# Twelve attention heads laid out as eight on 128 rows and four on 64 rows per image, in a kernel for a vision tower

## The chip, the core and the metric

The kernel runs on one core of one Trainium2 chip. The metric is the device time in microseconds (us) of the whole program. TensorE (PE in the profile) multiplies into eight banks of PSUM. VectorE (DVE), ScalarE (ACT) and GpSimd (POOL) do the work between the products, and SyncE (SP) issues most of the DMAs. The engines run on their own and meet at semaphores.

## What is computed

Sixty-four images of 3x224x224 become 196 tokens of 192 features each. A retention-like attention with twelve heads of 16 features follows (no softmax; the scores are multiplied by a decay with the distance), then a layer norm, a soft mixture of 64 slots with one two-layer expert each, and a last layer norm. Cut to what matters:

```python
h = einsum('bnk,dk->bnd', patches(x), W)                      # 196 tokens, K = 768, D = 192
q, k, v = silu(h @ Wq), silu(h @ Wk), silu(h @ Wv)            # 12 heads of 16
decay = where(i >= j, exp(log_slope[head] * (i - j)), 0)
out = ((q @ k.T) * decay) @ v                                 # per head
out = layernorm((out * sigmoid(h @ Wg1 @ Wg2)) @ Wo) * ln_w + ln_b
h = layernorm(h + out)
xn = rmsnorm(h) * norm_w;  logits = cosine(slots, xn) * scale
y = expert_s(softmax_over_tokens(logits) @ xn)                # 64 experts, 192 -> 768 -> 192
h = layernorm(h + softmax_over_slots(logits) @ y)
```

## The kernel before

The program has three phases. **Phase 1** goes over 32 pairs of images. A step i of it holds three stages of three different pairs: the tokens and the attention of pair i (flag `a`), the output projection and first norms of pair i-1 (`c`), the slot logits and slot inputs of pair i-2 (`d`). All 30 steps from 2 to 31 hold all three; steps 3 to 30 are a hardware loop. **Phase 2** runs the 64 experts, two at a time, with six weight buffers that SP refills. **Phase 3** combines, adds and normalises.

A pair has 392 token columns: two images of 196, each in two tiles of T = 98. The order of the work on each engine is that in which the code of `step` is written for it; nothing reorders it. TensorE's step reads: `embed(i, 0)`, `project_out(i-1, 0)`, `token_features(i-2)`, `embed(i, 1)`, `project_out(i-1, 1)`, `h_turned` with `logits` in it, the products for q, v and k, then the attention with pieces of pair i-2 set between its blocks.

The names that matter:

- Heads: two groups g of six heads (96 rows), so kT and qm are 96 x 2 x 392. An attention block is one (group, image), four to a pair (`ORDER`). `scores` (L1005) has 2 x 3 products, each of 32 rows (two heads, of whose queries `qm` holds one copy with the odd and one with the even head zeroed) into banks 2 to 4. `decay` (L801, DVE) multiplies the block by the decay into `p_sb` (L801, 98x1176). `values` (L1040) has 2 x 2 x 3 products that write 32 rows each. The next `scores` overwrites the banks, and so waits for the `decay` before it.
- The half of an image that attends to the other half across the tile border goes over a state: `keys_turned` (L1014), `kts` (DVE), `states` (L1023), `state` (DVE), `carried` (L1051), twelve products.
- q on ACT: two masked copies (L583, L584) and one plain one (`qs`, L586) per group; `zs` (L588) takes the 16 rows of the gate's first product, its low part is subtracted on DVE (L866, semaphore zl_rdy), and the second k product waits for that, since it overwrites the bank. `gate` (L961) makes two products, `gt` (L609) their tanh.
- `gated` (L807) writes `og`; ACT rounds it (`ogh`, L566), DVE subtracts (`ogl`, L840), and `project_out` makes 24 products of the split values (fp32r, three for one) with L945 to L947.
- `token_features` (L1073): 8 transposes. `logits` (L1083): 8 products. `logits_turned` (L1091), `dispatch_turned` (L1098), `slot_inputs` (L1106), `combine_turned` (L1066).
- A product of two fp32 operands shows as two records in the trace; a transpose and an fp32r product show as one. In the rows, 98*32 is rows by columns of the weights that are loaded.

Of the kernel before, what the change touches and what calls it, by code (L numbers as in the profile page):

```python
# [33 lines left out]
HG = H // 2  # L34
# [12 lines left out]
REGION = 34048  # L47
# [10 lines left out]
ORDER = [(0, 0), (0, 1), (1, 0), (1, 1)]  # L58

PAIRS = HG // 2  # L60
SC_AT = 2
V_AT = (4, 2)
LT_AT = 256


def vit_tower(nc, xT, W, Wq, Wk, Wv, Wo, Wg1, Wg2, log_slope, row_slope, ln_w, ln_b, slots, scale, fc1, fc1b, fc2, fc2b,
# [6 lines left out]
    with ExitStack() as ctx:  # L73
# [45 lines left out]
        kT = place("kT", [G, 2, PT])  # L119
        qm = place("qm", [G, 2, 2, PT])  # L120

        zs, gw = place("zs", [ZK, PT], F32R), place("gw", [ZK, D], F32R)
        kts = place("kts", [T, 2, D])
        wvh, wvl = place("wvh", [128, 2, D], F32R), place("wvl", [128, 2, D], F32R)
        qs, qd = place("qs", [G, 2, 2, T]), place("qd", [G, 2, 2, T])
        state = place("state", [G, 4, G])
        vpad = place("vpad", [T, 4, H * 32])
        dec = place("dec", [T, H, T])
        gt = place("gt", [G, 2, PT])
        p_sb = place("p_sb", [T, 2, 2, HG * T])  # L130
# [6 lines left out]
        wvst, wo = place("wvst", [128, 2, D]), place("wo", [G, 2, D])  # L137
        dist, steps = place("dist", [T, T]), place("steps", [G, T])
# [23 lines left out]
        og, ogh, ogl = sb("og", [G, 2, PT]), sb_r("ogh", [G, 2, PT]), sb_r("ogl", [G, 2, PT])  # L162
        woh, wol = sb_r("woh", [G, 2, D]), sb_r("wol", [G, 2, D])
        hb = sb("hb", [T, 4, D])
        t2 = sb("t2", [T, 4, D])
        gn = sb("gn", [T, 4, D])
        h2 = sb("h2", [T, 4, D])
        xn = sb("xn", [T, 4, D])
        tokT = sb("tokT", [G, 2, PT])

        slT = sb("slT", [G, 2, S])
        mask, parity = sb("mask", [G, HG]), sb("parity", [G, 2])
        slope, rslope = sb("slope", [T, H]), sb("rslope", [G, 2])
        left = sb("left", [T, 1])
        kdec = sb("kdec", [T, H])
        qdec = sb("qdec", [G, 2, T])
# [32 lines left out]
        qd_rdy, parity_rdy = sem("qd_rdy"), sem("parity_rdy")  # L209
# [9 lines left out]
        ogh_rdy, ogl_rdy = sem("ogh_rdy"), sem("ogl_rdy")  # L219
# [65 lines left out]
        def _(sp):  # L285
# [35 lines left out]
            def step(i, d):  # L321
                if d:
                    store_h2(i - 2)
                load_x(i + 2)
                if d:
                    store_comb(i - 2)
# [16 lines left out]
            sp.wait_ge(sc_mm, 4 * NP)  # L343
            load_weights(2, 2)
            store_comb(NP - 3)
            sp.wait_ge(pv_mm, 4 * NP)
# [11 lines left out]


# [8 lines left out]
            sp.wait_ge(h2_stored, 16 * NP)  # L368
            sp.wait_ge(comb_stored, 16 * NP)
            for n in range(DEEP):  # L370
                load_comb(n, n)
                load_h2(n, n)
# [168 lines left out]
        def _(act):  # L541
            act.wait_ge(first_loaded, 16 * N_FIRST)
            act.wait_ge(dist_st, 4)
            for h in range(H):
                act.activation(dec[:, h, :], dist[:, :], ACT.Exp, scale=slope[:, h:h + 1]).then_inc(dec_exp, 1)
# [777 lines left out]
```

## Time and profile before

| what | value |
|---|---|
| median of three runs | 1272.96 us (1271.07 to 1275.09) |
| the profiled execution | 1271.87 us, its span 1270.1 us |
| PE busy / DVE / ACT / POOL | 93% / 64% / 58% / 45% |
| phase 1, 2, 3 (PE's own stretches) | to 986 us, to 1164 us, to the end |
| steady step of phase 1 | 29.48 us |
| rounding `ogh` / subtracting `ogl`, mean of one of two per step | 525 ns / 560 ns |
| phase 2 | 5.50 us for two experts |
| phase 3 | 2.6 us for a pair, DVE without a pause |

The page's second part cuts the span into 40 slices of 31.8 us: a digit is a tenth. A timeline row has the start, the length from the first start to the last end, engine, line, what is written from what, and the number of records merged; in brackets the idle time before it and what ended it. Records of PE overlap, so the difference of two starts is what a group costs, not its length. PE's records stand nearly without a gap in phase 1, which makes the order and the spacing on PE the thing to read.

### The profile page before, as it was taken

To read this page: it belongs to the slowest core of one execution; us is meant where nothing else is said; L and a number is where in the kernel's file an instruction comes from. 1 tells how busy PE (TensorE), PEld (TensorE's weight loads), DVE (VectorE), ACT (ScalarE), POOL (GpSimd) and SP (SyncE) were. 2 spreads that over 40 slices of the span, in tenths; PEclk is the share of its full clock that TensorE was granted. 3 is DMA by queue.
4 is the path that set the end of the run, shared out by engine and by line. 5 is a ranking of instruction groups with operands and counts; after the bars stand their busy time and mean duration, and the time that the engine had idled before them with its cause. 6 is when DMAs were issued, how large, how long until landed. Compare 5 with 4: busy or idle time off the path is not lost.

```text
span 1270.1 us, 34978 instructions
## 1 busy us (share of the span) xinstructions
PE 1176.8 (93%) x12938; PEld 955.7 (75%) x12938; DVE 816.3 (64%) x2114; ACT 735.9 (58%) x1677; POOL 572.7 (45%) x878
## 2 busy tenths in 40 slices
PE   4999999999999999999999999999999999996653
PEld 4888888888888888888888888888887556553432
DVE  4677767677777777776767777777775122221897
ACT  5456667767667677666776766767753211110566
POOL 3355545455545455554545554555543000000664
PEclk8999999999999999999999999999999999999555
DMA  4411211111111111121111111111144699997686
GB/s 144 189 49 53 74 65 54 51 60 51 51 51 51 51 51 51 53 72 64 54 52 59 51 51 51 51 51 51 51 162 175 259 422 423 424 423 239 211 261 187
DMA packets 50653, 158.34 MB, mean 125 GB/s; under 512 B 5354, under 2 KB 31328, under 8 KB 38308
## 3 DMA queue, kind: packets, MB, share of 16 engines
q1 hardware_dynamic: 33016, 145.04, 31.0%
q10 hardware_dynamic: 17600, 12.78, 3.3%
q8 instruction: 27, 0.44, 0.1%
q14 instruction: 10, 0.08, 0.0%
HBM read 132.18 MB, written 25.62 MB: 124 GB/s over the span
## 4 chain that ended last, share of the span: by engine, by line
PE 78%; DVE 16%; issue 2%; ACT 1%; DMA 1%; SPq 1%; DVEq 1%; POOL 0%; ACTq 0%; POOLq 0%
PE ps L945 11%; PE ps L946 10%; PE ps L947 10%; DVE p_sb L801 7%; PE ps L1005 7%; PE ps L1040 6%; PE ps L1219 5%; PE ps L1238 4%; PE ps L1083 3%; PE ps L988 3%; PE ps L989 3%; PE ps L1023 2%; DVE res L914 2%; PE ps L1252 2%; PE ps L1243 2%; DVE st L920 2%
## 5 line engine op out<-in xcount | busy, mean ns | idle before, releaser
L423 POOL TENSOR_TENSOR xl<-x_sb,xh 128x392 fp32r<-128x392 f32 x192 | 189.2, 1017 | 86.1 <-DVE gn L776 77.9
L801 DVE TENSOR_TENSOR p_sb<-ps,dec 98x1176 f32<-98x1176 f32 x128 | 176.9, 1382 | 57.0 <-PE ps L1005 57.0
L1005 PE MATMUL ps<-qm,kT 32*98 32x196 f32 x1536 | 117.0, 343 | 9.6 <-DVE p_sb L801 7.6
L1040 PE MATMUL ps<-p_sb,vpad 98*32 98x98 f32 x3072 | 112.4, 250 | 1.9 <-DVE p_sb L801 1.9
L1040 PEld LDWEIGHTS ps<-p_sb,vpad 98*32 98x32 f32 x3072 | 84.5, 109 | 35.4 <-issue 24.7
L656 ACT ACTIVATE hg<-ps 128x768 f32<-128x768 f32 x32 | 26.0, 811 | 145.9 <-PE ps L1243 145.9
L1005 PEld LDWEIGHTS ps<-qm,kT 32*98 32x98 f32 x1536 | 75.2, 158 | 35.2 <-DVE p_sb L801 23.0
L906 DVE COPY y2st<-ps 128x192 f32<-128x192 f32 x32 | 11.4, 358 | 120.4 <-PE ps L1219 120.4
L1267 PE MATMUL ps<-y2b,cbuf 64*98 64x192 f32 x256 | 49.4, 538 | 41.8 <-POOL y2b L523 41.8
L673 ACT ACTIVATE o_sb<-res,nb,rstd 98x192 f32<-98x192 f32 x128 | 59.6, 536 | 48.6 <-DVE nb L929 47.9
L467 POOL TENSOR_TENSOR invn<-nrm,expo 98x4 f32<-98x4 f32 x32 | 32.7, 1023 | 117.4 <-DVE nrm L786 117.1
L740 DVE BATCH_NORM_STATS2 st<-ps 98x6 f32<-98x192 f32 x128 | 40.0, 354 | 70.4 <-PE ps L947 70.4
L945 PE MATMUL ps<-xl,wh 128*128 128x392 f32 x192 | 69.6, 363 | 12.4 <-POOL xl L423 12.3
L453 POOL TENSOR_TENSOR qd<-qs,qdec 96x196 f32<-96x196 f32 x64 | 36.4, 568 | 97.0 <-ACT qs L586 97.0
L442 POOL TENSOR_TENSOR hTl<-hT,hTh 128x392 fp32r<-128x392 f32 x32 | 32.7, 1022 | 101.6 <-ACT hTh L627 101.6
L553 ACT ACT_TABLE_LOAD x60 | 77.0, 1283 | 1.1
L1267 PEld LDWEIGHTS ps<-y2b,cbuf 64*98 64x98 f32 x256 | 32.6, 267 | 58.4 <-issue 47.2
L510 POOL CAST pickb<-pick 128x128 fp32r (+1 forms) x32 | 9.5, 296 | 148.7 <-PE ps L1243 148.7
L558 ACT ACTIVATE xh<-x_sb 128x1176 fp32r<-128x1176 f32 x64 | 71.7, 1168 | 0.8 <-DMA x_sb<-in_xT 0.8
L1219 PEld LDWEIGHTS ps<-w2v,hgT 128*64 128x64 f32 x768 | 52.3, 137 | 25.9 <-issue 18.5
L1219 PE MATMUL ps<-w2v,hgT 128*64 128x192 f32 x768 | 69.5, 330 | 1.1 <-DVE hgT L900 1.1
L491 POOL TENSOR_TENSOR xn<-gn,ra 98x192 f32<-98x192 f32 x128 | 68.0, 560 | 0.0
(186 smaller groups left out, 3627.6 us busy)
## 6 DMA issues: line engine op xcount, KB each, us to landing
x_sb<-in_xT SPq DMA_DIRECT2D x32, 1176.0 KB, 5.2
w1v<-in_fc SPq DMA_DIRECT2D x32, 1152.0 KB, 10.0
w2v<-in_fc SPq DMA_DIRECT2D x32, 1152.0 KB, 12.6
h_dram<-h SPq DMA_DIRECT2D x32, 294.0 KB
h2r<-h_dram SPq DMA_DIRECT2D x32, 294.0 KB
out<-o_sb ACTq DMA_DIRECT2D x32, 294.0 KB
comb_dram<-cst SPq DMA_DIRECT2D x32, 98.0 KB, 1.7
cbuf<-comb_dram SPq DMA_DIRECT2D x32, 98.0 KB, 4.0
```

The costliest lines, as they stand in the source:

```text
L423: pool.tensor_tensor(xl[:, k], x_sb[:, k], xh[:, k].bitcast(F32), ALU.subtract)\
L491: pool.tensor_tensor(xn[0:T, t], gn[0:T, t], amp[:, t:t + 1].to_broadcast([T, D]), ALU.mult)\
L553: act.activation(warm[:, 1:2], warm[:, 0:1], func)
L558: act.activation(xh[:, c], x_sb[:, c], ACT.Copy).then_inc(xh_rdy, 1)
L801: dve.tensor_tensor(dst, src, rate.unsqueeze(2).to_broadcast([T, PAIRS, 2, TOK]), ALU.mult)\
L945: pe.matmul(out, hi, x_lo, start=start, stop=False)
L946: pe.matmul(out, lo, x_hi, start=False, stop=False)
L947: return pe.matmul(out, hi, x_hi, start=False, stop=stop)
L1005: mm = pe.matmul(ps[0:T, SC_AT + r, mt * TOK:(mt + 1) * TOK].rearrange("p (b n) -> p b n", b=2), kT[rows, g, n], qm[rows, g, :, n], start= ...
L1040: mm = pe.matmul(ps[32 * b:32 * b + 32, 5 + g, a * TOK + mt * T:a * TOK + mt * T + T], vpad[:, 2 * a + mt, 32 * (g * HG + h):32 * (g * HG ...
L1219: mm = pe.matmul(ps[64 * s:64 * s + 64, 4 + n % 2, 0:D], hgT[:, k, at:at + 64], w2v[n][:, s, k], start=(k == 0), stop=(k == FJ - 1))
L1267: mm = pe.matmul(ps[0:T, 2 * n + a, k * D:(k + 1) * D], cbuf[64 * a:64 * a + 64, n, k * T:(k + 1) * T], y2b[64 * a:64 * a + 64, n, :], sta ...
```

## The change

Heads 0 to 7 (`HA`) of each image stand on 128 rows, heads 8 to 11 (`HB`) of both images on 64 rows each. There are three blocks for a pair: eight heads of image 0, eight of image 1, four heads of both, each with four products of 32 rows side by side into banks 2 to 5. `decay` is 98x1568, three times. Output and gate stand as 128 x 392 and 128 x 196. So the q, k and gate products write 128 and 80, 128 and 64, 128 and 64 rows, and ACT copies the 64-row parts for each image apart. `qs` is gone: POOL adds the two masked copies. Value rows of image 1 are computed after the first `scores` and the gate instead of before the k products. `ogh` and `ogl` are gone: `project_out` multiplies in fp32, once with 128 rows, and for the last four heads with 64 rows for each image. `token_features` and `logits` have the same split. The squares have a buffer of their own. Some banks move. On SP the load of the next x goes ahead of the stores, and the first four loads each of the combine weights and of h2 for phase 3 go ahead of the expert refills of phase 2.

```diff
-HG = H // 2
+HA = 8
+HB = H - HA
+DA, DB = HA * HD, HB * HD
+COLS = PT + TOK
...
-V_AT = (4, 2)
+V_AT = (2, 7)
...
             def step(i, d):
+                load_x(i + 2)
                 if d:
                     store_h2(i - 2)
-                load_x(i + 2)
-                if d:
                     store_comb(i - 2)
...
+            sp.wait_ge(h2_stored, 16 * NP)
+            sp.wait_ge(comb_stored, 16 * NP)
+            for n in range(DEEP):
+                load_comb(n, n)
+                load_h2(n, n)
             def slot_step(u, n):
...
-            sp.wait_ge(h2_stored, 16 * NP)
-            sp.wait_ge(comb_stored, 16 * NP)
-            for n in range(DEEP):
-                load_comb(n, n)
-                load_h2(n, n)
...
+                    for a in range(2):
+                        for b in range(2):
+                            last = act.activation(qB[DB * a:DB * a + DB, b], ps[0:DB, 1, a * TOK:(a + 1) * TOK],
+                                                  ACT.Silu, scale=parity[0:DB, b:b + 1])
+                    last.then_inc(q_sb, 1)
...
+                pe.matmul(ps[:, 0, 0:PT], gw[:, 0:DA], zs[:, :], start=True, stop=True).then_inc(g_mm, 1)
+                pe.matmul(ps[0:DB, 1, 0:PT], gw[:, DA:D], zs[:, :], start=True, stop=True).then_inc(g_mm, 1)
...
-                        mm = product(ps[0:T, 2 + x, (t % 2) * D:(t % 2) * D + D],
-                                     ogh[:, k, n], ogl[:, k, n], woh[:, k], wol[:, k], k == 0, k == 1)
+                for a in range(2):
+                    t = 2 * a + x
+                    pe.matmul(ps[0:T, SC_AT + 2 * x + a, 0:D], og[:, t * T:(t + 1) * T], wo[:, 0],
+                              start=True, stop=False)
+                for a in range(2):
+                    rows = slice(DB * a, DB * a + DB)
+                    mm = pe.matmul(ps[0:T, SC_AT + 2 * x + a, 0:D], og[rows, PT + x * T:PT + (x + 1) * T],
+                                   wo[rows, 1], start=False, stop=True)
...
-                    for r in range(PAIRS):
+                    for r in range(4):
                         rows = slice(32 * r, 32 * r + 32)
+                        keys, queries = (kA, qA) if k < 2 else (kB, qB)
```

On TensorE, from `embed` over `project_out` (wol, woh or wo) and `token_features` (gn) back to `embed`, the kernel before ends its twelve products of `project_out` so:

```order
L945 MATMUL ps<-wol,ogh 98x192
L946 MATMUL ps<-woh,ogl 98x192
L947 MATMUL ps<-woh,ogh 98x192
L1073 MATMUL ps<-ident,gn 96x98 x8
L988 MATMUL ps<-xl,whl 128x392
```

and in the changed kernel all of it is this, where L1006 and L1119 take all rows and columns of the array, L1010 has 64 rows and L1122 writes 64 rows:

```order
L966 MATMUL ps<-xh,wh 128x392
L1006 MATMUL ps<-wo,og 98x192 x2
L1010 MATMUL ps<-wo,og 98x192 x2
L1119 MATMUL ps<-ident,gn 128x98 x4
L1122 MATMUL ps<-ident,gn 64x98 x4
L1022 MATMUL ps<-xl,whl 128x392
```

Twelve fp32r products became four fp32 ones, and between the two `embed` the part of the array that a product takes changes four times instead of never. The same engine some 4 us later, around `logits` (slT), in the kernel before and then in the changed one:

```order
L1115 MATMUL ps<-ident,hT 98x128 x4
L1083 MATMUL ps<-slT,tokT 98x64 x8
L1117 MATMUL ps<-pick,hT 98x64 x4
```

```order
L1167 MATMUL ps<-ident,hT 98x128 x4
L1132 MATMUL ps<-slT,tokT 98x64 x2
L1135 MATMUL ps<-slT,tokT 98x64 x2
L1132 MATMUL ps<-slT,tokT 98x64 x2
L1135 MATMUL ps<-slT,tokT 98x64 x2
L1169 MATMUL ps<-pick,hT 98x64 x4
```

The eight products now alternate between all 128 rows (L1132) and 64 rows (L1135). TensorE's attention, from the first `scores` to the products before the last `values`, before:

```order
L1005 MATMUL ps<-qm,kT 98x196 x6
L1014 MATMUL ps<-ident,kT 98x96 x4
L961 MATMUL ps<-zs,gw 96x392 x2
L1091 MATMUL ps<-ident,Lt 64x98 x4
L1005 MATMUL ps<-qm,kT 98x196 x6
L1040 MATMUL ps<-p_sb,vpad 32x98 x12
L1023 MATMUL ps<-vpad,kts 96x96 x4
L1005 MATMUL ps<-qm,kT 98x196 x6
L1040 MATMUL ps<-p_sb,vpad 32x98 x12
L1098 MATMUL ps<-ident,Es 98x128 x2
L1051 MATMUL ps<-qd,state 32x98 x6
L1005 MATMUL ps<-qm,kT 98x196 x6
```

and after it, where twelve products of value rows (wvl, wvh) stand between L988 and L1051:

```order
L1043 MATMUL ps<-qA,kA 98x196 x8
L987 MATMUL ps<-zs,gw 128x392
L988 MATMUL ps<-zs,gw 64x392
L964 MATMUL ps<-wvl,hTh 98x192
```

```order
L1051 MATMUL ps<-ident,kA 98x128 x2
L1052 MATMUL ps<-ident,kB 98x128
L1143 MATMUL ps<-ident,Lt 64x98 x4
L1043 MATMUL ps<-qA,kA 98x196 x8
L1082 MATMUL ps<-p_sb,vpad 32x98 x16
L1060 MATMUL ps<-vpad,kts 128x128 x2
L1063 MATMUL ps<-vpad,kts 64x64 x2
L1043 MATMUL ps<-qB,kB 98x196 x8
L1082 MATMUL ps<-p_sb,vpad 32x98 x16
L1150 MATMUL ps<-ident,Es 98x128 x2
L1094 MATMUL ps<-qd,state 128x98 x2
L1158 MATMUL ps<-xn,DT 64x192 x4
```

One `scores` and one `values` are gone, half of the value rows and the changed gate stand after the first `scores`. ACT's order around q, before and after:

```order
L583 ACTIVATE qm<-ps,parity 96x392
L584 ACTIVATE qm<-ps,parity 96x392
L586 ACTIVATE qs<-ps 96x196
L588 ACTIVATE zs<-ps 16x392 x2
L593 ACTIVATE vpad<-ps 98x12x2x16 x2
```

```order
L588 ACTIVATE qA<-ps,parity 128x392
L589 ACTIVATE qA<-ps,parity 128x392
L592 ACTIVATE zs<-ps 16x392 x2
L595 ACTIVATE qB<-ps,parity 64x196 x4
L628 ACTIVATE vpad<-ps 98x12x2x16
```

Before, the first three rows stand twice, once for each group; now `zs` comes ahead of the four narrow q parts.

## Rows read from the trace of the kernel before

**Rows 1.** The page, second part: granted clock of TensorE, and DMA.
```profile
PEclk8999999999999999999999999999999999999555
GB/s 144 189 49 53 74 65 54 51 60 51 51 51 51 51 51 51 53 72 64 54 52 59 51 51 51 51 51 51 51 162 175 259 422 423 424 423 239 211 261 187
```
**Rows 2.** Timeline of PE: start, length, line, written from read, records; k to scores.
```profile
501.79 0.39 PE L945 MATMUL ps<-hTl,wkh 128*96 128x392 f32 x1
...
503.00 0.91 PE L1005 MATMUL ps<-qm,kT 32*98 32x196 f32 x12
...
504.67 0.56 PE L1091 MATMUL ps<-ident,Lt 98*64 98x98 f32 x8
505.41 0.91 PE L1005 MATMUL ps<-qm,kT 32*98 32x196 f32 x12 [0.18 <-DVE p_sb L801]
506.25 0.88 PE L1040 MATMUL ps<-p_sb,vpad 98*32 98x98 f32 x24
507.06 0.92 PE L1023 MATMUL ps<-vpad,kts 98*96 98x96 f32 x8
507.91 0.91 PE L1005 MATMUL ps<-qm,kT 32*98 32x196 f32 x12
```
**Rows 3.** Timeline of PEld, the weight loads: the first round of a scores block.
```profile
503.00 0.17 PEld L1005 LDWEIGHTS ps<-qm,kT 32*98 32x98 f32 x3 [0.29 <-issue]
```
**Rows 4.** Timeline of PE, the same step, end of the attention and next embed.
```profile
509.56 0.43 PE L1098 MATMUL ps<-ident,Es 128*98 128x128 f32 x2
...
512.18 0.87 PE L1106 MATMUL ps<-xn,DT 98*64 98x192 f32 x8
512.98 0.88 PE L1040 MATMUL ps<-p_sb,vpad 98*32 98x98 f32 x24
513.68 0.52 PE L1051 MATMUL ps<-qd,state 96*32 96x98 f32 x12
...
514.83 0.45 PE L945 MATMUL ps<-xl,wh 128*128 128x392 f32 x1
```
**Rows 5.** Timeline of PE, project_out, token_features, logits, and the next second k product.
```profile
518.15 0.25 PE L945 MATMUL ps<-wol,ogh 96*98 96x192 f32 x1
...
519.22 0.84 PE L1073 MATMUL ps<-ident,gn 98*96 98x98 f32 x8
519.84 0.42 PE L988 MATMUL ps<-xl,whl 128*128 128x392 f32 x1
...
523.57 1.52 PE L1083 MATMUL ps<-slT,tokT 96*98 96x64 f32 x16
524.93 0.86 PE L1117 MATMUL ps<-pick,hT 128*98 128x64 f32 x8
...
531.27 0.39 PE L945 MATMUL ps<-hTl,wkh 128*96 128x392 f32 x1
```
**Rows 6.** Timeline of ACT: the copy for the slot inputs, then q and zs.
```profile
510.03 0.38 ACT L638 ACTIVATE DT<-ps 98x256 f32<-98x256 f32 x1 [2.06 <-PE ps L1098]
...
526.92 0.58 ACT L583 ACTIVATE qm<-ps,parity 96x392 f32<-96x392 f32 x1 [1.40 <-PE ps L947]
...
527.88 0.32 ACT L586 ACTIVATE qs<-ps 96x196 f32<-96x196 f32 x1
528.10 0.59 ACT L583 ACTIVATE qm<-ps,parity 96x392 f32<-96x392 f32 x1
...
529.40 1.01 ACT L588 ACTIVATE zs<-ps 16x392 fp32r<-16x392 f32 x2
```
**Rows 7.** Timeline of DVE: a decay, and the low part of zs.
```profile
503.97 1.38 DVE L801 TENSOR_TENSOR p_sb<-ps,dec 98x1176 f32<-98x1176 f32 x1 [1.00 <-PE ps L1005]
...
530.45 0.57 DVE L866 TENSOR_TENSOR zs<-ps,zs 16x392 fp32r<-16x392 f32 x1 [0.83 <-ACT zs L588]
```
**Rows 8.** Groups by line: busy us, mean ns | idle before; a wide DVE operation.
```profile
L861 DVE TENSOR_TENSOR hb<-ps,lnb 98x768 f32<-98x768 f32 x32 | 30.5, 954 | 0.0
```
**Rows 9.** Timeline of POOL: the start of phase 3.
```profile
1174.73 2.23 POOL L523 TENSOR_TENSOR y2b<-y2r,b 128x192 f32<-128x192 f32 x4 [27.36 <-DMA y2r<-y_dram]
```

## What the change should do to the time

> **What bounds the kernel now.** I read the page's slices first. TensorE's granted clock is at its full level through phase 1 [rows 1], so lengths on PE can be carried over one for one. Phase 1 is 78% of the span, so the question is what sets its step. Two second k products lie 29.48 us apart (501.79 and 531.27 in [rows 2, 5]), and on the timeline of PE nearly every group starts where the one before it ends. The waits inside a step are 0.18 us before a `scores`, whose banks the `decay` still reads [rows 2], and about 0.25 us before the second k product, which needs `zs` and its low part. PE bounds the step, with DVE and ACT close behind at two places. Phases 2 and 3 run the same products after the change.
>
> **What a group costs on PE.** In a `scores` block three weight loads start together [rows 3]: three tiles of 32 rows work side by side. So a block with four tiles has the same number of rounds and costs the same; only a block less is a gain. The second thing to see is a price between groups. The 24 records of `values` cost 0.81 us when `states` follows (506.25 to 507.06 [rows 2]), and 0.70 us when `carried` follows, whose weights take the same part of the array (512.98 to 513.68 [rows 4]). The change of shape costs 0.11 us. `states` pays more on entering: 0.85 us for eight records [rows 2], while sixteen of `logits` between products of their own shape cost 1.36 us (523.57 to 524.93 [rows 5]), 0.085 each; that leaves 0.17 us. A change of shape is thus 0.11 to 0.17 us, since the first weights can't be loaded behind the products before. I take 0.15 us where rows or wide weights are concerned, 0.13 us else. The Trainium skill (TensorEngine Tiling (Array Packing), Key Properties) says that changing the tiling mode drains TensorE, without a price; it speaks against this change, and the 0.11 us above agrees with it. By the order the shape changes 17 times in a step before, and by my count 29 times after.
>
> **First half, from `embed` to q.** It is PE's alone.
> - `project_out`: before, twelve records of 192 columns, 1.07 us (518.15 to 519.22 [rows 5]). After, six rounds of 192 columns in fp32 (four with all rows, two with pairs of 64 rows). Four such rounds of `slot_inputs` cost 0.80 us with a change [rows 4], so (0.80 - 0.11) / 4 = 0.17 us at most, some of it the first load; I take 0.165. Six are 0.99, two changes 0.30: 1.29 us. That is 0.22 us more, twice.
> - `token_features`: before 0.62 us (519.22 to 519.84 [rows 5]). After, four transposes and four rounds at 0.084, 0.67 us, and two changes less what `embed` already paid, 0.25: 0.92 us, 0.30 more.
> - `logits`: before 1.36 us. After, eight records at 0.085, four rounds at 0.08, four changes: 1.60 us, 0.24 more.
> Together 0.98 us more for a step. ACT's two roundings and DVE's two subtractions of `og` go; they lay beside `embed`, so nothing comes of them here.
>
> **Second half, from q to the next `embed`.** I follow the path stretch by stretch, since waits decide here.
> - q to second k. Before: first q copy on ACT at 526.92, second k product at 531.27 [rows 5, 6], 4.35 us. After, ACT does two wide copies (until the second q product is there, 1.07), `zs` twice, 1.04, and four narrow copies, three at 0.22 from start to start and the last 0.33, as `qs` (527.88 to 528.10, length 0.32 [rows 6]); then the low part on DVE 0.04 and 0.57 [rows 7], and 0.25 from its end (531.02) to the product. That is 3.96 us, 0.39 less. PE would be free at 3.0, since half of the value rows has gone: it now waits 0.9 us instead of 0.25.
> - First to second `scores`. Before 2.41 us, of which PE's own work ends at 505.14 (504.67, four rounds of `logits_turned`, a change), so 2.14. After: the same, plus twelve value records like those of `project_out` before, 1.07, plus the gate's second product, now with 64 columns of weights between two full ones, two changes, 0.30: 3.51 us, 1.10 more. The `decay` needs less: 0.97 from `scores` to its start [rows 2, 7], its length, and 0.06. 98x1176 takes 1.38 [rows 7] and 98x768 0.954 [rows 8], 1.05 ns a column, so 98x1568 takes 1.79 us (1.84 if all of it scales): 2.82 us. So the value rows hide it, and no wait is left here.
> - Second to third `scores`. Before 2.50 us, all PE. After PE has 2.50 again, and the decay path 2.82: 0.32 more, now a wait on DVE.
> - Third `scores` to `embed`. Before 6.92 us (507.91 to 514.83 [rows 2, 4]). After: `scores` 0.84, `values` 0.81, then `dispatch_turned`, its copy on ACT 0.47 later [rows 4, 6], 0.38, and 0.05: 0.90, which hides the first `carried`; `slot_inputs` 0.80; then what was 1.85 (512.98 to 514.83), less two rounds of `carried`, plus a change, 1.80. Sum 5.15 us, 1.77 less. The third decay ends 0.4 us before its `values` asks for it.
> Together -0.39 + 1.10 + 0.32 - 1.77 = -0.74 us. The block that is saved comes back as new changes of shape and as value rows that no longer lie beside ACT's work on q.
>
> **The sum.** A step gets 0.24 us longer, 29.72 instead of 29.48; 30 full steps: +7.2 us. Steps 0 and 1 have no token work, so there four decays bounded the attention and now three do: by the same stretches -2.4 and -1.1, together -3.5. The closing steps have no `embed` that hides the rounding and subtracting of `og` (0.5 us each in the table, two of each, overlapping): -1.4, with 0.3 back for the added changes: -1.1. The four added exponentials at the start lie behind the loads, and a subtraction of the weights less gives nothing that I count. The moved loads on SP: 1.57 MB, 3.7 us at the 423 GB/s of the full slices [rows 1]. They leave the end of phase 2, where POOL waits 27.36 us for the slot outputs that PE's last products still have to deliver [rows 9]; that wait ends with a store after the last product. So between 0 and -3.7, I take -1. If their new place delays a refill it costs nothing, since in phase 2 SP waits for PE, not PE for loads. The x load moved on SP has over 10 us of room. POOL's two additions are about 0.6 us, ahead of a wait for the tokens. Sum: +7.2 - 3.5 - 1.1 - 1.0 = +1.6. The profiled span of 1270.1 becomes 1271.7, and the median of 1272.96, about 1.1 above that execution's time, becomes **1274.5 us**.
>
> **Rivals.**
> - *Faster: changes of shape are half hidden* where full products and 64-row pairs follow each other, for which the trace has no row. Twelve of them stand on PE's own stretches (ten in the first half, two at the gate): at half price -0.9 us a step, -27 us, 1247 us; for nothing, 1220 us. Against it: four kinds of change in the rows cost 0.11 to 0.17. Chance 0.16.
> - *Slower: ACT's narrow copies decide.* If each of the four q parts takes its full 0.33 instead of 0.22, and a switch of rows 0.1 more, the second k product comes 0.43 us later, and since PE already waits there, all of it lands on the step: +13 us, 1287 us. It decides as soon as ACT needs more than the 3.0 us at which PE is free, which it does by my sum already. Chance 0.2.
> - *Slower: the fourth tile is not free.* If a round of four tiles takes 4/3 of one with three, 0.22 us for 0.165 and 0.11 for 0.084, three `scores` and three `values` cost 1.3 us more a step, +40 us, 1314 us. For it: no row has four 32-row tiles. Against it: three start at once [rows 3]. Chance 0.05. The Trainium skill (TensorE: Matmul & The Clock Gate, Measured speedup vs the span model) gives 3.07 times for four row tiles; as an estimate by that page a round would be 1.3 times as long, which is this case, while its span model, some 4 ns for each tile more, gives my sum.
> - *Near my sum*, 0.59: its own range is 1265 to 1284.
>
> **How the numbers follow.** The step is a difference of terms of 1 us, multiplied by 30: an error of 0.03 us in the price of a change alone makes 11 us. A measurement can tell 0.3%, 3.8 us, from no change. Of the 0.59 about 0.16 lie under 1269.1, 0.28 between, 0.15 over 1276.8. With the rivals: faster 0.33 (0.01 of it from a larger gain at the moved loads), same 0.28, slower 0.39. The range leaves out the full form of the first rival and the third: 1253 to 1290.
>
> **What would show it.** In the profile after: a step of 29.7 us; three `scores` at 0.84 us; a wait of about 0.9 us before the second k product on ACT and DVE; a wait of 0.3 us before the third `scores`; `project_out` at 1.29, `token_features` at 0.92, `logits` at 1.60; a decay of 1.79. I am wrong if the pairs of 64 rows follow the full products without a gap, if four tiles take longer than three, or if the narrow copies take over 0.25 us each.

## The result, and the profile after

The kernel after takes 1277.97 us (median of 6 runs, 1277.40 to 1280.53), the kernel before beside it 1272.95 us (6 runs, 1271.07 to 1275.09). The ratio is 1.0047, 95% interval 1.0031 to 1.0063: the change makes the kernel 0.5% slower by this ratio, 5.0 us by the medians. The profiled execution has a span of 1276.0 us against 1270.1, so 5.9 us more. The prediction of 1274.5 us had the sign of its likeliest case right and was 3.5 us low; its own sum, +1.6 us, was smaller than the 3.8 us that it called measurable.

The page's row of the granted clock answers [rows 1]; it is the same, so everything else can be read in us.

```profile
PEclk8999999999999999999999999999999999999555
```

Next the timeline of PE over a step of the kernel after, cut to the groups that the prediction spoke of (start, length, line, written from read, records; in brackets the wait in front). It answers [rows 2, 4, 5].

```profile
507.66 0.36 PE L964 MATMUL ps<-hTl,wkh 128*64 128x392 f32 x1 [1.09 <-ACT qB L595]
508.85 0.92 PE L1043 MATMUL ps<-qA,kA 32*98 32x196 f32 x16
509.70 0.45 PE L987 MATMUL ps<-zs,gw 80*128 80x392 f32 x1
509.98 0.35 PE L988 MATMUL ps<-zs,gw 80*64 80x392 f32 x1
510.16 0.26 PE L964 MATMUL ps<-wvl,hTh 128*98 128x192 f32 x1
...
512.15 0.92 PE L1043 MATMUL ps<-qA,kA 32*98 32x196 f32 x16
513.00 0.88 PE L1082 MATMUL ps<-p_sb,vpad 98*32 98x98 f32 x32
513.81 0.71 PE L1060 MATMUL ps<-vpad,kts 98*128 98x128 f32 x4
...
514.98 0.92 PE L1043 MATMUL ps<-qB,kB 32*98 32x196 f32 x16 [0.19 <-DVE p_sb L821]
...
520.27 0.44 PE L964 MATMUL ps<-xl,wh 128*128 128x392 f32 x1
...
523.60 0.81 PE L1006 MATMUL ps<-wo,og 128*98 128x192 f32 x4
...
524.84 0.56 PE L1119 MATMUL ps<-ident,gn 98*128 98x98 f32 x4
...
529.79 0.48 PE L1132 MATMUL ps<-slT,tokT 128*98 128x64 f32 x4
...
531.33 0.91 PE L1169 MATMUL ps<-pick,hT 128*98 128x64 f32 x8
532.04 0.43 PE L964 MATMUL ps<-hTl,wqh 128*128 128x392 f32 x1
...
537.68 0.37 PE L964 MATMUL ps<-hTl,wkh 128*64 128x392 f32 x1 [1.09 <-ACT qB L595]
```

From one second k product to the next it is 30.02 us (507.66 to 537.68), 0.54 more than before; the prediction had 0.24 more. Two things can be seen at once. A `scores` block with four tiles takes 0.85 us (512.15 to 513.00), and `values` with 32 records 0.81 (513.00 to 513.81), as much as 24 records took [rows 2]. And in front of the second k product PE stands still for 1.09 us.

ACT's and DVE's timelines in front of that product show what it waits for. They answer [rows 6] and [rows 7].

```profile
533.39 0.59 ACT L588 ACTIVATE qA<-ps,parity 128x392 f32<-128x392 f32 x1 [1.92 <-PE ps L966]
533.88 0.58 ACT L589 ACTIVATE qA<-ps,parity 128x392 f32<-128x392 f32 x1
534.49 1.00 ACT L592 ACTIVATE zs<-ps 16x392 fp32r<-16x392 f32 x2
535.51 1.47 ACT L595 ACTIVATE qB<-ps,parity 64x196 f32<-64x196 f32 x4
...
537.01 0.56 DVE L886 TENSOR_TENSOR zs<-ps,zs 16x392 fp32r<-16x392 f32 x1 [0.97 <-ACT qB L595]
```

The four narrow q parts take 1.47 us where the prediction had 0.99. DVE then waits 0.97 us for the last of them, does the low part of `zs`, and only then PE goes on. That all of this chain lies on the path is tested below.

The other end of the sum is the turn from phase 2 to phase 3. The last copy of slot outputs on DVE and POOL's first addition (timeline of both, answering [rows 9]):

```profile
1175.60 0.36 DVE L925 COPY y2st<-ps 128x192 f32<-128x192 f32 x1 [2.34 <-PE ps L1263]
1180.86 2.23 POOL L531 TENSOR_TENSOR y2b<-y2r,b 128x192 f32<-128x192 f32 x4 [21.92 <-DMA y2r<-y_dram]
```

They are 5.26 us apart. Before, they were 10.69 us apart: that copy started at 1164.04 and the addition at 1174.73 [rows 9]. So the moved loads brought 5.4 us, and phases 1 and 2 together are 11.6 us longer (1175.60 against 1164.04).

### The profile page after: what moved, and what is told of

It is laid out like the page before. It is cut to its first block, busy times and chain, and to the rows that moved or that the text cites. A ratio compares the mean times of both kernels' runs of the same rounds, so it can differ in the third digit from the quotient of the medians.

```text
span 1276.0 us, 33496 instructions
## 1 busy us (share of the span) xinstructions
PE 1158.9 (91%) x12257; PEld 902.7 (71%) x12257; DVE 782.9 (61%) x2020; ACT 725.3 (57%) x1713; POOL 599.5 (47%) x942
## 4 chain that ended last, share of the span: by engine, by line
PE 72%; DVE 11%; ACT 11%; issue 3%; SPq 1%; DVEq 1%; DMA 1%; POOL 0%; ACTq 0%; POOLq 0%
PE ps L1043 7%; PE ps L964 6%; PE ps L966 5%; PE ps L965 5%; PE ps L1263 5%; DVE p_sb L821 5%; PE ps L1082 4%; ACT qB L595 4%; PE ps L1282 4%; PE ps L1006 3%; PE ps L1022 3%; PE ps L1023 3%; PE ps L1010 2%; ACT zs L592 2%; PE ps L1158 2%
## 5 line engine op out<-in xcount | busy, mean ns | idle before, releaser
L821 DVE TENSOR_TENSOR p_sb<-ps,dec 98x1568 f32<-98x1568 f32 x96 | 172.0, 1791 | 37.1 <-PE ps L1043 37.1
L1082 PE MATMUL ps<-p_sb,vpad 98*32 98x98 f32 x3072 | 85.0, 250 | 1.3 <-DVE p_sb L821 1.3
L1082 PEld LDWEIGHTS ps<-p_sb,vpad 98*32 98x32 f32 x3072 | 64.1, 109 | 26.3 <-issue 25.8
L635 ACT ACTIVATE h<-t,mur,ra 98x192 f32<-98x192 f32 x128 | 59.6, 537 | 38.8 <-DMA h_dram<-h 32.4
L964 PE MATMUL ps<-hTl,wkh 128*64 128x392 f32 (+1 forms) x128 | 45.0, 352 | 34.5 <-ACT qB L595 34.5
L779 DVE SCALAR_TENSOR_TENSOR t<-t,rstd,hb 98x192 f32<-98x192 f32 x128 | 60.4, 512 | 14.6 <-POOL rstd L482 14.6
L1022 PE MATMUL ps<-xl,whl 128*128 128x392 f32 x192 | 68.7, 358 | 0.0
```

The lines of the kernel that those rows point to most:

```text
L821: dve.tensor_tensor(dst, src, rate.unsqueeze(2).to_broadcast([T, 4, 2, TOK]), ALU.mult)\
L964: pe.matmul(out, hi, x_lo, start=start, stop=False)
L1022: pe.matmul(ps[:, 1, 0:PT], whl[:, k], xl[:, k], start=(k == 0), stop=False)
L1082: mm = pe.matmul(ps[32 * r:32 * r + 32, 6 + k // 2, at:at + T], vpad[:, 2 * a + mt, 32 * h:32 * h + 32], p_sb[:, k % 2, mt, (2 * r + odd) ...
```

## The experiments

One of the eleven kernels that follow is a change to the kernel before, ten are changes to the kernel after. Times are medians; each kernel was timed beside the kernel before on its chip (1272.02, 1272.45, 1271.43 and 1271.98 us in the four sets), and the ratios are to that. The kernel after, which has 1.0047 beside 1272.95, wasn't timed again in these sets.

**One part alone: the moved loads.** In the kernel before, only the eight loads are moved:

```diff
+            sp.wait_ge(h2_stored, 16 * NP)
+            sp.wait_ge(comb_stored, 16 * NP)
+            for n in range(DEEP):
+                load_comb(n, n)
+                load_h2(n, n)
             def slot_step(u, n):
...
-            sp.wait_ge(h2_stored, 16 * NP)
-            sp.wait_ge(comb_stored, 16 * NP)
-            for n in range(DEEP):
-                load_comb(n, n)
-                load_h2(n, n)
```

> The kernel before, with one part of the change alone: the eight first loads for phase 3 (comb and h2, 1.57 MB) stand ahead of the expert refills. As the trace of after reads, the last store copy and POOL's first addition of phase 3 then lie 5.3 us apart instead of 10.7, so the whole becomes 5.4 us shorter: about 1267.6 us. By the prediction's own term it is 1.0 us (1272), and its bound of 3.7 us would give 1269.3. If the gain in the trace of after comes from something else in the changed phase 1, this run stays at 1272.9.

Measured: 1265.79 us (7 runs), ratio 0.9945 (0.9926 to 0.9965), span 1264.1 instead of 1270.1. Not all of these 6 us are the loads'. From the last copy on DVE (1163.26) to POOL's first addition (1168.68) it is now 5.42 us instead of 10.69, so the loads bring 5.3 us. The second k product of step 2 came 0.7 us earlier too (88.42 us against 89.09), where both kernels run the same code: that much two executions can differ. The prediction's 1.0 us is refuted, and its bound of 3.7 us too. Why it is more than the bytes at full rate is seen in the DMA column of the windows around the end of phase 2. Columns: window, its length, busy time and count of PE, PEld, DVE, ACT, POOL, granted clock, share of the DMA engines, GB/s. First the kernel before, with SP's last issue of slot-output loads:

```profile
1162.00:1164.00 2.00, 1.93 (x24) 1.41 (x20) 0.00 (x0) 0.00 (x0) 0.00 (x0) 1.00 0.57 207
1166.00:1168.00 2.00, 0.00 (x0) 0.00 (x0) 0.00 (x0) 0.00 (x0) 0.00 (x0) 1.00 0.57 212
...
1170.91 1.40 SPq L377 DMA_DIRECT2D y2r<-y_dram  x4
```

Then e1_loads_alone, the same columns, and the same issue on SP:

```profile
1162.00:1164.00 2.00, 1.15 (x16) 0.72 (x10) 0.36 (x1) 0.00 (x0) 0.00 (x0) 1.00 0.10 42
1165.36 1.40 SPq L377 DMA_DIRECT2D y2r<-y_dram  x4
```

In both kernels the engines move 225 and 226 GB/s from 1150 to 1160, less than the 423 of the refills [rows 1]; now they carry the slot outputs. Why the rate is only half wasn't tried. In the kernel before, the eight loads stand ahead of the slot outputs in the queue, so about 1.57 MB more were still to be moved at 1160, and at 210 GB/s these take 7.5 us (an estimate from the rows). About 2 of them would cost nothing, since in e1 the queue is nearly empty from 1162 on and the last copy comes only at 1163.26; the rest is near the 5.3 us measured. The last stores of slot outputs have to get through that, and SP can issue the last four loads only when they have landed: 6.87 us after the last copy (1164.04 to 1170.91) instead of 2.10 (1163.26 to 1165.36). That is 4.8 of the 5.3 us. That the stores were slow because of the loads around them is read from these rows; no run took it apart further.

**ACT's and DVE's chain in front of the second k product.** In the kernel after, one wait on DVE is changed, so that the low part of `zs` lies beside the narrow copies:

```diff
-                    dve.wait_ge(q_sb, 2 * i + 2)
+                    dve.wait_ge(zh_rdy, 2 * i + 2)
                     dve.tensor_tensor(zs[ZL:ZL + RANK, :], ps[DB:DB + RANK, 1, 0:PT], zs[0:RANK, :].bitcast(F32),
```

> After, with one wait changed: DVE's low part of zs waits for the two zs copies on ACT (zh_rdy) instead of the four narrow q copies behind them (q_sb). Theory A, ACT's narrow copies and DVE's low part in a row hold up the second k product: the low part (0.56 to 0.60 us) then lies beside the narrow copies, the product starts about 0.1 us after the last of them, a step is 0.6 us shorter, the whole 18 us: about 1260 us. Rival B, the wait before the second k product has slack behind it (the step is set by TensorE's groups and the decays, and a gain there comes back as a wait before a scores block): within 4 us of 1278.

Measured: 1258.67 us (4 runs), ratio 0.9890 (0.9856 to 0.9924). PE's timeline, two blocks a step apart and the second k product between them:

```profile
501.92 0.92 PE L1043 MATMUL ps<-qA,kA 32*98 32x196 f32 x16
...
526.81 0.40 PE L964 MATMUL ps<-hTl,wkh 128*64 128x392 f32 x1 [0.45 <-ACT qB L595]
...
531.32 0.92 PE L1043 MATMUL ps<-qA,kA 32*98 32x196 f32 x16
```

The step is 29.40 us, 0.62 less than in the kernel after, and the wait has gone from 1.09 to 0.45. Rival B falls: of the 0.64 us that the wait lost, 0.62 came off the step, so nothing behind it had slack.

**The price of a narrow copy, on the path.** A fifth copy behind the four:

```diff
+                    last = act.activation(spare[DB:2 * DB, :], ps[0:DB, 1, TOK:PT], ACT.Silu, scale=parity[0:DB, 1:2])
                     last.then_inc(q_sb, 1)
```

> After, with a fifth narrow q copy of 64x196 behind the four, into a scratch tile that nobody reads. Theory A (1.47 us for four, so 0.37 us each, all of it on the path): +0.37 us a step, 32 steps, +12 us: 1290 us. If a narrow copy costs 0.22 us from start to start, as the prediction took: +7 us, 1285. Rival B (slack behind the wait): within 4 us of 1278.

Measured: 1287.56 us (4 runs), ratio 1.0114 (1.0080 to 1.0148), and in the trace

```profile
512.77 0.36 PE L966 MATMUL ps<-hTl,wkh 128*64 128x392 f32 x1 [1.41 <-ACT spare L598]
...
543.09 0.37 PE L966 MATMUL ps<-hTl,wkh 128*64 128x392 f32 x1 [1.40 <-ACT spare L598]
```

The step is 30.32 us, 0.30 more; the wait grew by the same 0.31. So a narrow copy costs the step what it costs ACT, 0.31 us here, between the 0.37 of theory A (which had divided 1.47 by four) and the 0.22 of the prediction. By the times it is 9.6 us over the kernel after in 32 steps, 0.30 each. Why it is 0.3 and not 0.22 is seen on the four copies one by one, on ACT's timeline of the kernel after:

```profile
535.51 0.42 ACT L595 ACTIVATE qB<-ps,parity 64x196 f32<-64x196 f32 x1
535.84 0.41 ACT L595 ACTIVATE qB<-ps,parity 64x196 f32<-64x196 f32 x1
536.26 0.42 ACT L595 ACTIVATE qB<-ps,parity 64x196 f32<-64x196 f32 x1
536.58 0.40 ACT L595 ACTIVATE qB<-ps,parity 64x196 f32<-64x196 f32 x1
```

From start to start 0.33 (same output rows), 0.42 (the output moves from rows 0 to 63 to rows 64 to 127, and the overlap is gone), 0.32, and the last has its length, 0.40. The groups by line, which give the mean ns of one shape, add the second half of the answer (the kernel after: line, names, shapes, count, busy us, mean ns, idle before):

```profile
L595 ACT ACTIVATE qB<-ps,parity 64x196 f32<-64x196 f32 x128 | 46.5, 412 | 1.2
L603 ACT ACTIVATE kB<-ps 64x196 f32<-64x196 f32 x64 | 20.9, 326 | 35.0 <-PE ps L966 34.6
L589 ACT ACTIVATE qA<-ps,parity 128x392 f32<-128x392 f32 x32 | 18.5, 580 | 0.0
L600 ACT ACTIVATE kA<-ps 128x392 f32<-128x392 f32 x32 | 15.7, 490 | 0.0
L592 ACT ACTIVATE zs<-ps 16x392 fp32r<-16x392 f32 x64 | 31.4, 490 | 2.4 <-PE ps L966 0.9
```

The same shape takes 412 ns with the column `parity` as its scale and 326 without; 580 and 490 for the wide one. The column costs 0.09 us. The Trainium skill (ScalarE: Activation LUTs, What ACT_TABLE_LOAD costs) says just that: 93 ns for each pointer operand, and 93 ns of overlap between activations in a row. The rows agree with both: 0.086 and 0.090 us for the column, 0.08 to 0.09 of overlap. Where the output moves to other rows there is no overlap. With the third `qB` copy the source moves as well, but the two `zs` copies read the same source, write rows 0 to 15 and then 64 to 79, and take 1.00 us together (534.49 above) for 490 ns each; and the two copies to `tokT`, from one bank and then another into the same rows, start 0.39 us apart (525.93 and 526.32) though the first is 0.50 long. So it is the output rows and not the source.

**The column taken away.** The four copies with a number for scale (the zeroing of every second head's rows in `qB` is left out):

```diff
                             last = act.activation(qB[DB * a:DB * a + DB, b], ps[0:DB, 1, a * TOK:(a + 1) * TOK],
-                                                  ACT.Silu, scale=parity[0:DB, b:b + 1])
+                                                  ACT.Silu, scale=1.0)
```

> After, with the four narrow q copies scaled by the number 1.0 instead of the column of parity (this leaves out the zeroing of every second head's rows in qB). Theory: the column costs 0.09 us a copy (in after 64x196 takes 412 ns with a column, 326 without; 128x392 580 and 490), and copies to the same rows overlap by some 0.09. So the four take 0.24 + 0.33 + 0.24 + 0.33 = 1.14 us instead of 1.47, all of it on the path: -0.33 us a step, 32 steps, -10.5 us: 1267.5. Rival: the copies are longer because they are narrow, or because they read one bank four times, and not by the column: 1278 within 2.

Measured: 1266.85 us (7 runs), ratio 0.9956 (0.9940 to 0.9972), and ACT's timeline has

```profile
529.66 1.10 ACT L595 ACTIVATE qB<-ps 64x196 f32<-64x196 f32 x4
```

1.10 instead of 1.47 us, and the wait in front of the second k product is 0.72 instead of 1.09. The rival falls: it is the column. This explains 0.37 of the 0.48 us that the four copies took over the prediction's 0.99; the rest is the lost overlap, for which there was no run of its own.

**The value rows put back.** The second half of the value rows between the two k products instead of behind the gate:

```diff
                     project(i, 0, wkh, wkl, k_mm)
+                    pe.wait_ge(hb_sb, i + 1)
+                    rows_of_v(i, 1)
                     pe.wait_ge(q_sb, 2 * i + 2)
...
                     gate(i)
-                    pe.wait_ge(hb_sb, i + 1)
-                    rows_of_v(i, 1)
```

> After, with one move undone: TensorE does the second half of the value rows (twelve products, 1.07 us) between the two k products instead of behind the gate, so that they lie beside ACT's narrow copies. Theory A: the wait of 1.1 us before the second k product is filled, that product starts where it did (within 0.1 us), and from the first to the second scores block the path is now the decay: 2.8 us instead of 3.3. A step is 0.45 us shorter, the whole 14 us: about 1264 us. The prediction's reading, with 0.9 us of wait, gives the same sign. Rival C, the place is right because the value rows hide the decay, which otherwise has to be waited for in full: within 4 us of 1278, or slower.

Measured: 1265.69 us (7 runs), ratio 0.9938 (0.9914 to 0.9961). PE's timeline:

```profile
531.12 0.36 PE L964 MATMUL ps<-hTl,wkh 128*64 128x392 f32 x1
...
532.29 0.92 PE L1043 MATMUL ps<-qA,kA 32*98 32x196 f32 x16
...
535.13 0.92 PE L1043 MATMUL ps<-qA,kA 32*98 32x196 f32 x16 [0.33 <-DVE p_sb L821]
```

The profile names no wait in front of the k product any more. It still starts 0.11 us after DVE's low part of `zs` ends (531.01) and 4.29 us after the first q copy (526.83), as in the kernel after, and the value rows lie beside that chain. From the first to the second `scores` it is 2.84 us instead of 3.30: now the decay ends last there. The step is 29.53 us (502.76 to 532.29). The second half of the rows thus fills a wait that the kernel after has to bear in any case, and rival C falls.

**The order of `logits`.** All four products with 128 rows first, then the four pairs:

```diff
                 for x in range(2):
                     at = slice(LG_AT + S * x, LG_AT + S * x + S)
                     for a in range(2):
                         t = 2 * a + x
-                        pe.matmul(ps[0:T, 6 + a, at], tokT[:, t * T:(t + 1) * T], slT[:, 0, :], start=True, stop=False)
+                        pe.matmul(ps[0:T, 6 + a, at], tokT[:, t * T:(t + 1) * T], slT[:, 0, :], start=(x == 0),
+                                  stop=False)
+                for x in range(2):
+                    at = slice(LG_AT + S * x, LG_AT + S * x + S)
                     for a in range(2):
                         rows = slice(DB * a, DB * a + DB)
                         mm = pe.matmul(ps[0:T, 6 + a, at], tokT[rows, PT + x * T:PT + (x + 1) * T], slT[rows, 1, :],
-                                       start=False, stop=True)
+                                       start=False, stop=(x == 1))
```

> After, with the eight products of logits in another order: all four with 128 rows first, then the four pairs of 64 rows, so that TensorE changes its shape twice there and not four times. Theory A, a change costs 0.11 to 0.17 us and this stretch is on the path: logits takes 1.54 - 0.26 = 1.28 us, a step 0.26 us less, 30 steps: -8 us, 1270. Rival B, the pairs follow the full products without a price of their own and the 1.54 us are the products themselves: 1278 +- 2. Rival C, the gain comes back in the wait before the second k product: also 1278, but with a shorter logits in the trace. C is unlikely, since that wait is counted from the first q product, which also comes earlier.

Measured: 1270.45 us (10 runs), ratio 0.9987 (0.9972 to 1.0001). PE's timeline:

```profile
525.60 0.82 PE L1132 MATMUL ps<-slT,tokT 128*98 128x64 f32 x8
526.36 0.56 PE L1138 MATMUL ps<-slT,tokT 64*98 64x64 f32 x8
526.85 0.91 PE L1172 MATMUL ps<-pick,hT 128*98 128x64 f32 x8
```

The group takes 1.25 us instead of 1.54, with the same sixteen records. Two changes of shape less are 0.29 us, 0.145 each, between products for which the trace of before had no row. The time is 7.5 us under the kernel after, for 30 x 0.29 = 8.7. The first rival of the prediction, that full products and pairs follow each other for less, is refuted by this.

**The repairs together.** e6_early_and_half_rows has the wait of e2_low_part_early and puts six of the twelve value products between the k products; e7_half_rows_grouped adds the order of `logits`:

```diff
+                    pe.wait_ge(hb_sb, i + 1)
+                    rows_of_v(i, 1, (0,))
                     pe.wait_ge(q_sb, 2 * i + 2)
...
                     gate(i)
-                    pe.wait_ge(hb_sb, i + 1)
-                    rows_of_v(i, 1)
+                    rows_of_v(i, 1, (1,))
```

> After, with the low part of zs waiting for zs alone (as in e2_low_part_early) and half of the second value rows, six products, 0.53 us, between the two k products. Theory A: in e2 0.45 us of wait are left before the second k product, which these six products fill, so it starts where it did there; from the first to the second scores block the decay decides, 2.84 us as in e4_v_rows_early, instead of 3.30. A step is 28.95 us, the whole 14 us under e2: about 1244 us. Rival B, the two gains are the same time counted twice (in e4 too the product waited for ACT): within 4 us of 1258.7.

Measured: 1245.95 us (4 runs), ratio 0.9787 (0.9761 to 0.9813).

> The two together: e6_early_and_half_rows with logits in the order of e5_logits_grouped. Theory A: -8 us on e6, about 1236 us. If one of the other engines bounds the first half by now, it stays at e6's time.

Measured: 1238.30 us (4 runs), ratio 0.9734 (0.9709 to 0.9759). The step is 28.93 us in e6 and 28.64 in e7. On PE's timeline of e7 the profile names no wait in front of the second k product and the first two `scores`:

```profile
516.33 0.39 PE L964 MATMUL ps<-hTl,wkh 128*64 128x392 f32 x1
...
517.53 0.92 PE L1044 MATMUL ps<-qA,kA 32*98 32x196 f32 x16
...
520.37 0.92 PE L1044 MATMUL ps<-qA,kA 32*98 32x196 f32 x16
...
523.20 0.92 PE L1044 MATMUL ps<-qB,kB 32*98 32x196 f32 x16 [0.19 <-DVE p_sb L821]
```

So e7 beats the kernel before by 2.7% and the kernel before with the moved loads alone (0.9945) by 2.1%. Not all of the 2.1% need be the packing's: the kernel before wasn't given the same care. Its step has waits of 0.18 and about 0.25 us on PE, so filling both would bring it at most 13 us, 1.0% (an estimate, not run). About half of the 2.1% is then left to the packing at least.

**One step further, which failed.** In e7 two more changes of shape can be saved, if the pairs of the second `project_out` go right ahead of the pairs of `logits`:

```diff
                 if c:
                     project_out(i - 1, 1, d_before)
...
                     logits(i - 2)
+                if c:
+                    out_pairs(1)
+                if d:
+                    logits_pairs()
```

> e7_half_rows_grouped, and the pairs of 64 rows of the second project_out moved behind the full products of logits, right ahead of the pairs of logits: two changes of shape less. By the price of a change -0.26 us a step, -8 us on e7: about 1228 us. Rival: DVE gets the second project_out some 0.9 us later, has only 0.64 us of wait left before the logits, and hands on the rest to hb, for which the early value rows wait on TensorE: 0 to +5 us on e7.

Measured: 1252.99 us (4 runs), ratio 0.9848 (0.9823 to 0.9874), 14.7 us over e7: outside both expectations, the rival's 5 us too. PE's timeline shows both the gain and its end:

```profile
515.09 0.81 PE L1007 MATMUL ps<-wo,og 128*98 128x192 f32 x4
...
518.47 0.43 PE L964 MATMUL ps<-hTl,wqh 128*128 128x392 f32 x1
...
523.66 0.34 PE L964 MATMUL ps<-wvl,hTh 128*98 128x192 f32 x1 [0.65 <-DVE hb L881]
524.30 0.36 PE L964 MATMUL ps<-hTl,wkh 128*64 128x392 f32 x1
```

From the second `project_out` to q it is 3.38 us, in e7 3.68, so the two changes did bring 0.30. But from q to the second k product it is 5.83 us, in e7 5.00, since the value rows wait for `hb`, and DVE, which got the product of `project_out` later, works without a pause until `hb` is done. The next two kernels ask whether it is `hb` alone: on DVE it goes ahead of the last residual_statistics,

```diff
                 if c:
                     residual(i - 1, 1)
-                    residual_statistics(i - 1, 1)
...
                         .then_inc(hb_sb, 1)
+                if c:
+                    residual_statistics(i - 1, 1)
```

> e8_pairs_together with one operation moved on DVE: hb (0.96 us), for which the early value rows on TensorE wait, goes ahead of the last residual_statistics (0.85 us) instead of behind them. Theory: in e8 the two changes of shape less did save 0.30 us a step, and a new wait of 0.65 us for hb before the early value rows (with 0.15 in what follows) ate it. Then hb is done 0.85 us earlier, the wait goes and the step is 28.35 us: 0.3 under e7_half_rows_grouped, about 1230 us. Rival: DVE is late as a whole, not hb alone, so the low part of zs or the tokens, now behind, delay the second k product or the first decay: 1236 to 1250 us.

> Control to e9: e7_half_rows_grouped with hb ahead of the last residual_statistics, and the pairs where they were. No wait for hb stands in e7's trace, so nothing is to be gained: 1238 us, within 3. If it comes out at 1230 as well, the gain of e9 is not that of the changes of shape.

Measured: 1254.30 us for e9 (4 runs, ratio 0.9864, 0.9840 to 0.9887), and 1238.06 for e10 (4 runs, 0.9730, 0.9711 to 0.9749). The control stays at e7's time, as expected. In e9 the wait for `hb` is gone, and another of the same size stands behind it. DVE's and PE's timelines:

```profile
524.23 0.56 DVE L888 TENSOR_TENSOR zs<-ps,zs 16x392 fp32r<-16x392 f32 x1
524.89 0.36 PE L966 MATMUL ps<-hTl,wkh 128*64 128x392 f32 x1 [0.70 <-issue]
```

The profile names nothing as the releaser ("issue"), but the product starts 0.10 us after the low part of `zs` ends at 524.79. My theory of e9 falls and its rival holds in its mechanism, though the time lies 4 us over the rival's 1250: DVE is late as a whole. It starts on the second `project_out` 0.91 us before the first q product (518.08 and 518.99), in e7 1.72 us before it (509.61 and 511.33), and then works without a pause until the low part of `zs` is done. The order of its operations only decides which product of PE has to wait.

## Why the prediction was right, and by how much by luck

The profiled span is 5.9 us longer, the sum had 1.6. Taken by its steps:

- **First half, from `embed` to q: right.** Predicted 0.98 us more; measured 1.00 (520.27 to 532.04 is 11.77, before 10.77). In part that is luck: the four terms came to 0.87, and 0.13 stands in the second `embed`, the transposes of h and the `pick` group, 0.04 to 0.05 each, which the sum had unchanged. `project_out` takes 1.24 (523.60 to 524.84; predicted 1.29), `token_features` 0.97 (to the next `embed` at 525.81; 0.92), `logits` 1.54 (1.60). The price of a change of shape, 0.11 to 0.17, was measured again by e5 as 0.145.
- **q to second k: wrong by 0.33 us in the term of the narrow copies.** Predicted 3.96 us from the first q copy, measured 4.29 (533.39 to 537.68). The wide copies and `zs` are as predicted (1.10 and 1.02 for 1.07 and 1.04), the handing on by DVE is 0.70 for 0.86, and the four narrow copies are 1.47 for 0.99. I had taken 0.22 from start to start from `qs` [rows 6], a copy that has no column as its scale and had the overlap. Theirs is 0.33, and 0.42 where the output rows change. The trace of before had what was wanted: `qm` with a column takes 585 ns, `kT` without one 495, both 96x392. The second rival's sizes, 0.33 and 0.1 for a switch of rows, are what came. e2, e3 and e11 show that this chain is on the path: the step followed it by -0.62, +0.30 and -0.38 us.
- **First to second `scores`: 0.21 us less than predicted** (3.30 for 3.51). The gate's two products take 0.46 (509.70 to 510.16), before it was 0.51 for two of the same shape; I had added 0.30 for the changes around the second one, which has 64 columns of weights. It starts 0.28 after the first and hands on after 0.18 us, as products with 392 columns and full weights do on this timeline, so its two changes don't show. The transposes are 0.42 (511.24 to 511.66), 0.1 more than before. Why these changes are free and those of `logits` are not wasn't tried.
- **Second to third `scores`: right** (2.83 for 2.82, with the decay at 1791 ns), and the wait on DVE stands there, 0.19 us for the 0.3.
- **Third `scores` to `embed`: 0.14 us more** (5.29 for 5.15), of it 0.09 between `dispatch_turned` and `slot_inputs` (516.65 to 517.64, 0.99): the copy on ACT takes the 0.38 predicted, but `slot_inputs` starts 0.15 after its end, not 0.05.
- The step is then 0.54 us longer instead of 0.24, in 30 steps 16.2 us instead of 7.2.
- **The moved loads: wrong.** -1.0 was taken, with -3.7 as a bound; -5.4 is what they brought, -5.3 alone (e1). The step that failed is the price: the bytes at the rate of the refills. The trace has them moved at 210 GB/s, the rate of the slot outputs that they push past the end, and the last stores landed only in that traffic.
- Steps 0 and 1 and the closing steps: predicted -4.6 together. What is left of the span, 5.9 - 16.2 + 5.4, is -4.9. The split is less good. The second k product of step 2 stands 1.5 us earlier than before (87.58 and 89.09) with 0.97 of that step's own lengthening already in it, so steps 0 and 1 gave about -2.5 for the predicted -3.5. From that of step 31, which is 13.9 us later (957.82 and 943.93), to the last copy of phase 2, 11.6 later, it is -2.3; the step's own change behind that product is -0.4 of it, and about -1.9 is left for the predicted -1.1. Each is known to 0.7 us only, as e1 shows.
- The load of x on SP and POOL's two additions had no run of their own.

So the time came near because two errors went against each other: the sum had 9.0 us too little for the steps, and for the loads a gain that was 4.4 us too small. The sign too was luck in part: a sum of +1.6 us hardly speaks for slower, and the prediction gave slower a chance of 0.39. Of the rivals, the second (narrow copies) happened in its mechanism and nearly in its size: 0.33 us a step for its 0.43. The time stayed 9.4 us under its 1287, 4.4 of it by the loads and 3.9 by a step that got 0.54 us longer and not 0.67. The first is refuted by e5. The third, that the fourth tile isn't free, is refuted by the `scores` and `values` above. The Trainium skill (TensorE: Matmul & The Clock Gate, Measured speedup vs the span model) gives 3.07 times for four row tiles with 512 columns; here, with 196 columns, four take the time of three, as its span model has it.

## What to carry to other kernels

A packing that saves work on the busiest engine moves it to the engines that unpack; before it is made, the chain of copies in front of the next product is to be added up with the operands they will have, and whatever else the busiest engine has to do belongs into the wait that this chain leaves. Here the packing, with the moved loads, was 0.5% slower with that wait open and 2.7% faster with it filled and the `logits` regrouped. The loads for phase 3 were better issued before the traffic that everybody waits for, and their price was not their bytes at full rate but the time for which they held up the last transfer.

## What the runs showed of the hardware that I had not expected

- An activation with a column of SBUF as its scale takes 0.09 us longer than one with a number (412 and 326 ns for 64x196, 580 and 490 for 128x392, and 320 for the same copy in e11).
- Activations in a row overlap by 0.09 us when they write the same rows, and not when the output moves to other rows (0.33 and 0.42 us from start to start for `qB`; 0.39 for `tokT`, 0.50 long, against 1.00 for two of `zs`, 0.49 long each).
- Sixteen 32-row products with four tiles side by side take 0.85 us, as twelve with three took 0.84 [rows 2].
- A change of shape costs 0.145 us between full products and pairs of 64 rows (e5), but nothing that shows around a single product with 64 columns of weights (509.98 to 510.16, 0.18 us, between two with more).
